# Gate, up and down projections on one core: a chunk pair's fourth operand cast one product later, and a passage to the down projection with sooner loads and waits per bank

## What is computed

```python
mod = (silu(c) @ wmod).reshape(2, 6, 1, 1024)        # sa, ca, ga, sb, cb, gb
h = layernorm(x) * (1 + ca) + sa
x = x + ga * attn(h)             # one softmax over the batch of 2 per feature, h added
h = layernorm(x) * (1 + cb) + sb
gate, up = silu(h @ W_gate.T), h @ W_up.T            # 1024 -> 2752
x = x + gb * ((gate * up) @ W_down.T)                # 2752 -> 1024
```

## Time and profile before

| | |
|---|---|
| median of three runs | 2738.33 us |
| the profiled execution | 2740.02 us, its span 2738.2 us |
| PE busy | 2630.4 us of the span, 96% |
| DVE, ACT, POOL busy | 1800.6, 1306.2, 181.3 us |
| mean granted clock of PE | 0.976 |
| gate and up products | until 1887 us |
| down projection | from 1893 us to the end |
| DMA | 228 GB/s over the span |

### The profile page before, as it was taken

How to read it: one execution, slowest core, us unless ns; L and a number is a source line. 1 busy time by engine, 2 the same in 40 slices (tenths; PEclk the granted TensorE clock), 3 DMA queues, 4 the chain that set the end, 5 groups by cost and what they waited for, 6 DMA issues and landing times. The chain is left out here.

```text
span 2738.2 us, 33610 instructions
## 1 busy us (share of the span) xinstructions
PE 2630.4 (96%) x11968; PEld 2130.1 (78%) x11968; DVE 1800.6 (66%) x2507; ACT 1306.2 (48%) x2058; POOL 181.3 (7%) x225
## 2 busy tenths in 40 slices
PE   6578999999999999999999999999999999999999
PEld 3237888887888887888887888887888888888887
DVE  7988777866677757677767666665545555545544
ACT  4566456545456655466655333333433433333442
POOL 6500011010011010011000000000000000000000
PEclk8679999999999999999999999999999999999999
DMA  8675666557666558665558877878657658657655
GB/s 340 250 309 162 193 221 216 197 173 253 196 223 214 174 173 287 197 223 191 197 157 303 271 251 244 264 237 287 239 214 280 213 204 285 223 202 265 238 198 171
DMA packets 291285, 625.35 MB, mean 228 GB/s; under 512 B 22192, under 2 KB 91824, under 8 KB 285232
## 3 DMA queue, kind: packets, MB, share of 16 engines
q1 hardware_dynamic: 272400, 550.85, 59.0%
q0 software_dynamic: 17088, 59.78, 6.5%
q10 hardware_dynamic: 1632, 12.58, 1.1%
HBM read 437.79 MB, written 185.34 MB: 228 GB/s over the span
## 5 line engine op out<-in xcount | busy, mean ns | idle before, releaser
L1723 PE MATMUL ps<-x_hi_P,w_hi 128*128 128x512 f32 x2416 | 944.1, 391 | 18.8 <-DVE x_lo_P L1209 7.5
L1724 PE MATMUL ps<-x_lo_P,w_hi 128*128 128x512 f32 x2416 | 942.6, 390 | 0.0
L1725 PE MATMUL ps<-x_hi_P,w_lo_P 128*128 128x512 f32 x2416 | 942.2, 390 | 0.0
L762 ACT CAST w_hi<-w_raw_P 128x512 fp32r<-128x512 f32 x604 | 374.0, 622 | 438.8 <-PE ps L1725 423.4
L1192 DVE TENSOR_TENSOR w_lo_P<-w_raw_P,w_hi 128x512 fp32r<-128x512 f32 x604 | 413.4, 685 | 210.0 <-PE ps L1725 186.2
L1723 PEld LDWEIGHTS ps<-x_hi_P,w_hi 128*128 128x128 f32 x2416 | 454.9, 188 | 118.2 <-issue 12.5
L1725 PEld LDWEIGHTS ps<-x_hi_P,w_lo_P 128*128 128x128 f32 x2416 | 454.9, 188 | 95.2
L1724 PEld LDWEIGHTS ps<-x_lo_P,w_hi 128*128 128x128 f32 x2416 | 455.1, 188 | 93.1
L1786 PE MATMUL ps<-hh,w_hi 128*128 128x512 f32 x1232 | 480.6, 390 | 6.8 <-DVEq L1394 5.7
L1787 PE MATMUL ps<-hl,w_hi 128*128 128x512 f32 x1232 | 480.3, 390 | 0.0
L1788 PE MATMUL ps<-hh,w_lo 128*128 128x512 f32 x1232 | 480.0, 390 | 0.0
(11 more groups left out here) (189 smaller groups left out, 2037.7 us busy)
## 6 DMA issues: line engine op xcount, KB each, us to landing
w_raw_P<-wgu SPq DMA_DIRECT2D x294, 256.0 KB, 2.9
w_raw_P<-wsum_dram SPq DMA_DIRECT2D x252, 256.0 KB, 3.5
hl_raw<-h_dram SPq DMA_DIRECT2D x84, 768.0 KB, 7.4
w_raw<-wds_dram SPq DMA_DIRECT2D x64, 704.0 KB, 4.6
h_dram<-hb SPq DMA_DIRECT2D x33, 1280.0 KB, 5.6
w_raw<-wdn SPq DMA_DIRECT2D x48, 704.0 KB, 5.0
wsum_dram<-w_raw_P SPq DMA_DIRECT2D x84, 256.0 KB, 3.0
x_raw_P<-xr_dram SPq DMA_DIRECT2D x21, 1024.0 KB, 11.9
```

The source lines that it names most:

```text
L762: s.copy(w_hi[m % HI_RING][:], w_raw[(name, u)][:]).then_inc(whi_ready, 1)
L1723: mm(to, hi[:, w], xh, start=fresh and k == 0, stop=False, skip_group_check=not fresh)
L1724: mm(to, hi[:, w], xl, start=False, stop=False, skip_group_check=not fresh)
L1725: ins = mm(to, lo[:, w], xh, start=False, stop=k == KH - 1, skip_group_check=not fresh)
```

## The change

Between two pairs the cast of P2 moves on ACT from i = 10 of the last group to i = 1 of the next, the cast of P7 from 0 to 2; on DVE the rest of P2 moves from i = 0 to 2 and that of P7 from 2 to 3. P3 and P4 stay.

In the last group of all, SP loads h in two halves at i = 2 and 4 in place of 5, stores `th` at i = 7 in place of 10, and loads the weight of b = 3 and the h of stage 1 as soon as all products are done, ahead of the last store of h; the waits for the stores of h stand before the first load that reads what they wrote. DVE does `down_sums` at i = 3, `t_sums_first` at 5, the rest of weight 0 at 4, of pieces 0, 1 and 2 at 6, 7 and 8, and of piece 3 at i = 9 before `finish_mixed`; ACT casts weight 0 at 4, the pieces at 5, 6, 7 and 8, and weight 1 at 9. PE waits per bank: block 0 only for P4's bank (`h1_done` one less), block 1 for `n_done`, block 2 for `c11_done`, block 4 for `c12_done`. ACT's waits for the stores move to the first copies that overwrite what is stored. The arithmetic is the same.

```diff
--- before.py
+++ after.py
@@ -426,6 +426,8 @@
                 sp.dma_start(h_dram[s, 0:kept, :, p, :].rearrange("c p t -> p c t"), hb[:, 0:kept]).then_inc(h_stored[0], 16)
                 if s:
                     sp.dma_start(h_dram[s, 5:7, :, p, :].rearrange("c p t -> p c t"), ww[:]).then_inc(h_stored[1], 16)
+
+            H_LOAD_AT = {2: (0, 1), 4: (2, 3)}
 
             def load_h(stage, c):
 
@@ -491,7 +493,7 @@
                         else:
                             sp.wait_ge(h_stored[0], 16 * NPT)
                         sp.dma_start(th[:, 0:4], h_dram[0, 0:4, :, p, :].rearrange("c p t -> p c t")).then_inc(th_loaded, 16)
-                    if i == 10:
+                    if i == (7 if p == NPT - 1 else 10):
                         sp.wait_ge(th_ready, p + 1)
                         for i_, name_ in ((1, "P5"), (4, "P7"), (3, "P6"), (2, "P4")):
                             sp.dma_start(h_dram[0, H_SLOT[name_], :, p, :], th[:, i_]).then_inc(th_stored, 16)
@@ -502,9 +504,9 @@
                     if p == NPT - 1:
                         if i == 2:
                             load_w2(0)
-                        if i == 5:
-                            sp.wait_ge(prod_done, m + 1)
-                            for c in range(len(H_PIECES)):
+                        if i in H_LOAD_AT:
+                            sp.wait_ge(prod_done, m)
+                            for c in H_LOAD_AT[i]:
                                 load_h(0, c)
                         if i == 7:
                             sp.wait_ge(prod_done, m + 1)
@@ -512,10 +514,13 @@
                         if i == 10:
                             sp.wait_ge(th_stored, 16 * 4 * NPT)
                             load_w2(2)
+            sp.wait_ge(prod_done, M_ALL)
+            load_w2(3)
+            for c in range(len(H_PIECES)):
+                load_h(1, c)
             store_h(NS * NPT - 1)
             sp.wait_ge(ds_stored, 16 * NPT)
             sp.wait_ge(th_stored, 16 * 4 * NPT)
-            sp.wait_ge(prod_done, M_ALL)
 
             def load_y(e):
 
@@ -537,17 +542,16 @@
 
             for e in range(2):
                 load_y(e)
-            for half in range(2):
-                sp.wait_ge(h_stored[half], 16 * NPT * (NS - half))
             for b in range(NBLK):
                 stage, q = b // NQ, b % NQ
-                if b + 3 < NBLK:
-                    if b:
-                        sp.wait_ge(blk_done, b)
+                if q == 0 and stage + 1 == len(STAGES):
+                    for half in range(2):
+                        sp.wait_ge(h_stored[half], 16 * NPT * (NS - half))
+                if b and b + 3 < NBLK:
+                    sp.wait_ge(blk_done, b)
                     load_w2(b + 3)
-                if q == 0 and stage + 1 < NSTAGE:
-                    if stage:
-                        sp.wait_ge(blk_done, NQ * stage)
+                if b and q == 0 and stage + 1 < NSTAGE:
+                    sp.wait_ge(blk_done, NQ * stage)
                     for c in range(len(H_PIECES)):
                         load_h(stage + 1, c)
                 e = evac_before(b)
@@ -894,7 +898,7 @@
                 act.wait_ge(xp_loaded[name], 16 * s_)
                 s.copy(x_hi[name][:], x_raw[name][:]).then_inc(xhi_ready, 1)
 
-            X_HI_AT = {7: "P1", 8: "P5", 9: "P6", 10: "P2"}
+            X_HI_AT = {7: "P1", 8: "P5", 9: "P6"}
 
             def h_hi_cast(stage, c):
 
@@ -937,21 +941,18 @@
                         prep(s_, r, m - group_base(s_, r))
                     if p == NPT - 1 and i in X_HI_AT:
                         x_hi_cast(s_ + 1, X_HI_AT[i])
-                if s_ and p == 0 and i in (0, 3, 4):
-                    x_hi_cast(s_, {0: "P7", 3: "P3", 4: "P4"}[i])
+                if s_ and p == 0 and 1 <= i <= 4:
+                    x_hi_cast(s_, ("P2", "P7", "P3", "P4")[i - 1])
                 if g == NS * NPT - 1:
-                    if i == 5:
+                    if i == 4:
                         w2_hi_cast(0)
-                    for c in {8: (0,), 9: (1,), 10: (2, 3)}.get(i, ()):
-                        h_hi_cast(0, c)
-                    if i == 10:
+                    if 5 <= i <= 8:
+                        h_hi_cast(0, i - 5)
+                    if i == 9:
                         w2_hi_cast(1)
             silu_c12(NS * NPT - 1, 0)
 
             act.wait_ge(h2_done, NS * NTILE)
-            for half in range(2):
-                act.wait_ge(h_stored[half], 16 * (NS - half) * NPT)
-            act.wait_ge(ds_stored, 16 * NPT)
 
             for b in range(NBLK):
                 stage, q = b // NQ, b % NQ
@@ -965,10 +966,15 @@
                 if name == "P6":
                     if s_:
                         act.wait_ge(y_done, 4 * NQ * (s_ - 1) + 2 * NQ + q + 1)
+                    elif q == 0:
+                        for half in range(2):
+                            act.wait_ge(h_stored[half], 16 * (NS - half) * NPT)
                     s.copy(qv[q][:], bank_q[q]).then_inc(qv_copied, 1)
                 if name == "P7":
                     if s_:
                         act.wait_ge(y_done, 4 * NQ * (s_ - 1) + NQ + q + 1)
+                    elif q == 0:
+                        act.wait_ge(ds_stored, 16 * NPT)
                     s.copy(qw[q][:], bank_q[q]).then_inc(qw_copied, 1)
                 if b + 2 < NBLK:
                     w2_hi_cast(b + 2)
@@ -1453,6 +1459,8 @@
                 if g == 0:
                     x_first(i)
                 if p == NPT - 1 and i == 9:
+                    if s == NS - 1:
+                        h_lo_part(0, 3)
                     finish_mixed(g)
                 if i == 12:
                     finish_second(g, 0)
@@ -1476,17 +1484,17 @@
                         prep(s, r, m - group_base(s, r))
                     if p == NPT - 1 and i in X_LO_AT:
                         x_lo_part(s + 1, X_LO_AT[i])
-                elif i == 5:
+                elif i == (3 if p == NPT - 1 else 5):
                     down_sums(p)
-                elif i == 7:
+                elif i == (5 if p == NPT - 1 else 7):
                     t_sums_first(p)
-                if s and p == 0 and i in (0, 2, 4, 5):
-                    x_lo_part(s, {0: "P2", 2: "P7", 4: "P3", 5: "P4"}[i])
+                if s and p == 0 and 2 <= i <= 5:
+                    x_lo_part(s, ("P2", "P7", "P3", "P4")[i - 2])
                 if g == NS * NPT - 1:
-                    if i == 5:
+                    if i == 4:
                         w2_lo_part(0)
-                    for c in {8: (0,), 9: (1,), 10: (2, 3)}.get(i, ()):
-                        h_lo_part(0, c)
+                    if 6 <= i <= 8:
+                        h_lo_part(0, i - 6)
                     if i == 10:
                         w2_lo_part(1)
             finish_second(NS * NPT - 1, 0)
@@ -1751,14 +1759,18 @@
                             sum_over_features((ps_mean_g, ps_var_g)[i], NGRP * s + r, i)
                 product(m)
 
-            pe.wait_ge(h1_done, NS * NTILE)
-            pe.wait_ge(c11_done, NS * NTILE)
-            pe.wait_ge(c12_done, NS * NTILE)
-            pe.wait_ge(n_done, NS)
             for b in range(NBLK):
                 stage, q = b // NQ, b % NQ
                 s, name = stage // len(STAGES), STAGES[stage % len(STAGES)]
                 c = NQ * s + q + 1
+                if b == 0:
+                    pe.wait_ge(h1_done, NS * NTILE - 1)
+                if b == 1:
+                    pe.wait_ge(n_done, NS)
+                if b == 2:
+                    pe.wait_ge(c11_done, NS * NTILE)
+                if b == NQ:
+                    pe.wait_ge(c12_done, NS * NTILE)
                 if name == "P1" and s:
                     pe.wait_ge(y_done, 4 * NQ * (s - 1) + 3 * NQ + q + 1)
                 if name == "P2" and s:
```

## The result

The change takes 2721.89 us (median of four runs, 2721.29 to 2726.44) against 2739.58 us before (four runs): ratio 0.9944, 95% interval 0.9932 to 0.9956. The forecast was 2721 us, between 2716 and 2729.

The account below looks back on a forecast made before the run. PE, busy 96%, bounds the kernel, so only its gaps and low-clock stretches can be won: 4.9 + 3.0 + 1.0 + 8.2 = 17.1 us off 2740.0, set against the 2738.3 median, gives 2721 us, range 2716 to 2729.

Parts of the forecast that it names:

- Price of a gap: PE's waits in the four passages: each costs its row plus 0.25 us, sometimes low clock too; together 21.5 us.
- First passage, 4.9 us won: First passage between chunk pairs: DVE has no down_sums or t_sums there, so all 4.9 us are won.
- Second, 3.0: Second passage between chunk pairs: DVE has i = 9's weight just in time; 3.0 of 3.3 us won, at worst 1.
- Third passage, 1.0: Third passage between chunk pairs: DVE's work bounds it, a 2.7 us gap at i = 9; 1.0 us won, between 0 and 3.7.
- I take another 1.6 us off: Third passage: the 2.7 us gap at i = 9 is followed by PE's low clock, costing 1.6 us.
- the step that gave 0.6 back: Third passage: the small waits behind i = 9, for DVE's next weights, are gone, winning some 0.6 us.
- The passage to the down projection, 8.2: Last group to down projection: PE starts 1.3 us late, no low clock, 1.4 of 9.6 us left; 8.2 us won.
- the store of group 42: Last group: two h pieces queued ahead delay this store, awaited by ACT's copy of P7's bank, by 2 us (0 to 4.3).
- rival 1: Last group: h pieces issued behind group 42's store share the queue and delay it; 3 us less won, 2724; chance 0.14.
- Rival 2: Second and third passages: DVE bounds both, second gets a low-clock gap, third wins nothing; costs 4, 2725; chance 0.10.
- Rival 3: Three passages: the wait only moves, DVE's total work held PE; 8.9 us less won, 2730; chance 0.06.
- Rival 4: Three passages: ACT holds i = 6's weight while P2 lands some 10 us later; slower, 2744; chance 0.03.

Follow-up runs that it names:

- the kernel with the operand part alone: The kernel before with only P2's and P7's casts and rests moved, the last group untouched: 2731.71 us, ratio 0.9977.
- the last kernel: The change plus, in the third passage, later sums and their two 1 MB loads behind group 32's store, and piece 2's rest behind P4's finish: 2716.09 us, ratio 0.9911.
- the kernel with the passage alone: The change with P2's and P7's moves undone, so only the last group and the passage to the down projection differ from before: 2729.01 us, ratio 0.9968.

## Why the prediction was right

**Price of a gap, and the four passages.** Right, with one term missing. Nothing outside the passages moved. The row's gap plus 0.25 us fits: the kernel with the operand part alone wins 5.0 in the first passage for 4.9, and 3.3 in the second for 3.3 (the gap of 0.62 us at i = 2 cost only 0.65). But the sum of 21.5 leaves out the gap of 0.93 us at i = 9 of the third passage, 1.2 us with its 0.25, and so the last kernel could win 22.9. Also, the wait of 6.5 us is the largest entry after 300 us, not the largest but one.

**First passage, 4.9 us won.** 5.0 (4.3, and 0.65 of the new gap at 1059.43). **Second, 3.0.** 3.3 less the 0.65: 2.6. That gap at i = 2 was not foreseen. It is not the operand's work: it is 0.28 to 0.93 us in the second passage of some of the other kernels and absent in others (in the kernel with the passage alone it is 0.62 us in the third passage), and it stands behind the chain P5's load, its cast and rest, P3's finish. It goes with ACT's waits for the loads of P1 and P5 ahead of it: together they are 1.06, 1.11, 1.40, 1.40 and 1.73 us where the gap is 0.28, 0.34, 0.62, 0.62 and 0.93, and at most 0.93 us where there is none. Why these loads land sooner or later stays open.

**Third passage, 1.0.** 0.85, by two terms that failed and happened to cancel: forecast were 2.0 up to i = 9, less 1.6, plus 0.6; measured are 2.2, 0 and -1.3. That the total fits is luck. The step with DVE as the bound was right in place and size: a gap of 2.7 us at i = 9 was forecast, 2.6 was measured between starts. The step "I take another 1.6 us off" for the low clock was wrong for this profile, and too dear in itself: in the kernel with PE's waits together it did follow the same gap, and cost 0.5 net; and the step that gave 0.6 back for the weights behind i = 9 missed a wait: DVE waited 1.95 us for ACT's copy of P7's bank, ACT for the store of group 32, and PE got gaps of 0.26 and 0.87 us at i = 10 and 11. The sum watched the store in the last group only, though the same copy waits for a store in each group of the last three pairs. In the third passage SP issues that store 11.7 us after the first matmul of i = 2, against 7.6 in the second. It had done so before the change as well (12.0), but there PE came later and the wait did not show.

**The passage to the down projection, 8.2.** 9.1 (5.2 at its start, 3.9 behind). The mechanism was as forecast, for both steps, and the two kernels with the waits put back show their prices there: 7.8 and 8.4 us. The term that was mis-sized is the store of group 42, 2 us later by the sum:

```profile
1873.06 0.59 ACT L851 COPY ww<-ps 128x512 f32<-128x512 f32 x1 [1.43 <-DMA h_dram<-ww]
...
1882.36 0.68 DVE L1395 TENSOR_TENSOR hb<-ps,p 128x512 f32<-128x512 f32 x1
...
1890.97 0.59 ACT L965 COPY q<-ps 128x512 f32<-128x512 f32 x1 [2.59 <-PE ps L1800]
```

Taken from the start of the last product's last matmul, the copy is 9.15 us ahead of it, and was 9.88 ahead before: 0.7 us later, which DVE, busy until 1874.1, did not feel. Without the wait the sum had P4's finish 0.15 us behind that matmul's start, and it is there, at 1882.36. So half of the h loads ahead of the store and half behind it harmed little; which is also the end of rival 1, that had the copy some 5 us later. The rule on starts in order within one queue was not put to a test of its own.

**Rival 2** (both later passages bound by DVE) holds for the third alone. **Rival 3** falls: the operand part by itself gives 8.2 us. **Rival 4** falls: the cast of P2 waits in no passage of the change for its load. The mean granted clock is 0.979, a little above 0.976 as forecast.

## What to carry to other kernels

A wait for several things at a stage's start is worth splitting by what the first block really touches, but only together with the next wait behind it: here either of two waits put back alone cost nearly the whole gain, 7.8 and 8.4 of 9.1 us. A copy that must wait for a store of the stage before is a hidden cost of every load queued ahead of that store: a wait that is half covered in one profile is the next bound when the first one goes. Likewise a stretch of low clock ahead of another bound costs less than its own length, here 0.5 and nothing in place of 1.6 us. To compare kernels that differ by a few us, measure from a common matmul behind the noisy opening to the end of the span.

## What the runs showed of the hardware

The length of a gap does not tell whether PE's clock falls behind it. Gaps of 3.06 and 1.82 us were followed by the 1.2 GHz level before the change (granted clock 0.50 or 0.51), and gaps of 3.31, 2.47, 1.93 and again 1.82 us in other kernels were not (1.00); one of 2.48 us was in one kernel (0.50), and almost the same gap at the same place was not in three others (2.46, 2.47 and 2.49). The four gaps over 5 us behind the opening (5.71 twice, 5.97, 5.37) all were, for some 7 to 14 matmuls at 0.43 us, at 1.6 to 2.9 us of lost time. So only behind such a gap did the low clock come every time; 1.6 us behind one of 2 to 3 us is a chance.
